# First maxima in every second expert of the last chunk, the mixed output's products split, and the second attention's first weights split in the gate's network

## What is computed

```python
xn = layernorm(x)
q, k, v = (split(lora_linear(xn, ...)) for ...)        # 16 heads of 16, full attention
s = lora_linear(softmax(q @ k.T * 0.25) @ v, Wo, ...)
x_lat = xn @ fc1.T                                     # mixture of 32 experts, 8 per token
h = relu2(einsum('tl,eil->eti', x_lat, w1)) * cw
routed = einsum('eti,eli->tl', h, w2) @ fc2.T
shared = relu2(xn @ shared_up.T) @ shared_down.T
x = x + s * silu(shared + routed)
xn = layernorm(x)
s = attention(xn)                                      # 32 heads of 64, 30 of them local, 2 global
x = x + s * silu((sigmoid(xn @ Q(w1).T) * (xn @ Q(w2).T)) @ Q(w3).T)   # Q: ternary weights
```

## Time and profile before

| | us |
|---|---|
| median of 3 runs | 3155.75 (3152.42 to 3157.56) |
| the profiled execution | 3153.2 |
| its span, first to last instruction | 3151.4 |
| PE busy in it | 3000.4 (95%) |
| DVE, ACT, POOL busy | 2127.0 (67%), 1864.5 (59%), 993.8 (32%) |
| stage 1 (`first_half`) | 0 to 684.4 |
| stage 2 (`first_attention`) | 684.4 to 1449.0 |
| stage 3 (`gate_network`) | 1449.0 to 1626.5 |
| stage 4 (`second_attention`) | 1626.5 to 3151.4 |

### The profile page before, as it was taken

One profiled execution on the slowest core, in us unless ns is written; L12 is line 12 of the kernel. 1 busy time (PEld: TensorE's weight loads), 2 busy tenths in 40 slices (PEclk: granted clock), 3 DMA queues, 4 the chain that ended last, 5 costly groups with the idle time before them and its releaser, 6 DMA issues. The chain is left out here.

```text
span 3151.4 us, 66399 instructions
## 1 busy us (share of the span) xinstructions
PE 3000.4 (95%) x23634; PEld 2263.2 (72%) x23634; DVE 2127.0 (67%) x5897; ACT 1864.5 (59%) x4638; POOL 993.8 (32%) x1607
## 2 busy tenths in 40 slices
PE   7999999989999999996988999999999999999998
PEld 5888888854444444434877888788887888788886
DVE  5666666679989989976755555555556555565556
ACT  4666666648877777783435555455554555545553
POOL 0000000000000000002016666576655766566663
PEclk9999999989999999998999999999999999999999
DMA  4111111142233143102224444354343444244432
GB/s 150 49 48 48 48 48 41 44 84 41 54 50 70 29 76 47 30 7 100 97 83 109 104 95 96 98 127 103 83 118 88 117 103 93 66 116 108 101 87 69
DMA packets 296707, 246.35 MB, mean 78 GB/s; under 512 B 149180, under 2 KB 231740, under 8 KB 296252
## 3 DMA queue, kind: packets, MB, share of 16 engines
q1 hardware_dynamic: 296380, 242.11, 31.7%
HBM read 100.71 MB, written 44.04 MB: 46 GB/s over the span
## 5 line engine op out<-in xcount | busy, mean ns | idle before, releaser
L1804 ACT ACTIVATE b_pp<-b_pp,b_nm 128x192 f32<-128x192 f32 (+2 forms) x1024 | 472.9, 463 | 448.5 <-DVE b_nm L1972 367.0
L974 ACT ACTIVATE a_pt<-ps 128x512 f32<-128x512 f32 x1024 | 556.1, 595 | 169.8 <-PE ps L1006 168.8
L176 DVE TENSOR_REDUCE mx<-ps 128x2 f32<-128x1024 f32 x512 | 621.4, 1224 | 50.7 <-PE ps L167 36.3
L1774 POOL TENSOR_SCALAR b_pp<-b_pp,b_rc 128x192 f32<-128x192 f32 x960 | 388.6, 432 | 383.4 <-DVE b_rc L1981 383.4
L1993 DVE COPY b_pt<-ps 128x384 f32<-128x384 f32 (+2 forms) x336 | 182.0, 555 | 317.7 <-PE ps L1893 302.4
L1972 DVE CUSTOM_DVE_ANT_0 b_pp<-ps,b_mk 128x192 f32<-128x192 f32 x960 | 276.4, 354 | 133.4 <-PE ps L1872 133.4
L800 DVE SCALAR_TENSOR_TENSOR f_yac<-ps,f_cw,f_yac 128x128 f32<-128x128 f32 x992 | 278.1, 343 | 128.1 <-PE ps L604 125.7
L959 POOL TENSOR_TENSOR a_s<-a_s,g 128x256 f32<-128x256 f32 x32 | 23.4, 731 | 879.0 <-DVE a_s L1070 879.0
L604 PEld LDWEIGHTS ps<-w,f_sq 128*128 128x128 f32 x2048 | 265.7, 191 | 25.4 <-issue 5.1
L604 PE MATMUL ps<-w,f_sq 128*128 128x128 f32 x2048 | 269.7, 275 | 0.3
L1927 PE MATMUL ps<-b_wo,b_oT 128*128 128x256 f32 x1024 | 241.6, 380 | 3.7 <-ACT b_vv L1797 3.7
(11 more groups left out here) (269 smaller groups left out, 7310.6 us busy)
## 6 DMA issues: line engine op xcount, KB each, us to landing
b_rt<-b_qf SPq DMA_DIRECT2D x1024, 64.0 KB, 2.0
qk_parts<-f_aa SPq DMA_DIRECT2D x32, 512.0 KB, 2.7
v_rows<-f_va_ SPq DMA_DIRECT2D x16, 512.0 KB, 2.8
b_raw<-in_W1qT SPq DMA_DIRECT2D x64, 128.0 KB, 2.6
b_raw<-in_W1kT SPq DMA_DIRECT2D x64, 128.0 KB, 2.7
b_vraw<-in_W1vT SPq DMA_DIRECT2D x32, 256.0 KB, 3.2
b_wo<-in_W1oT SPq DMA_DIRECT2D x16, 512.0 KB, 4.0
b_vs<-b_vv SPq DMA_DIRECT2D x60, 128.0 KB, 2.8
```

The costliest lines, as they stand in the source:

```text
L176: e.tensor_reduce(M["mx"][kh % 3][:, :, jt, h], P.pair(s), AX.X, ALU.max, negate=True).then_inc(P.free_sem(s), 1)
L974: e.activation(pt[(4 * i + 2 * j + a) % 12][:, :], P.ap((*s, a)), ACT.Exp).then_inc(P.free_sem((*s, a)), 1)
L1774: m = e.tensor_scalar(x, x, r[:, 2 * u + h:2 * u + h + 1], 1.0, ALU.mult, ALU.mult)
L1804: e.activation(x, x, ACT.Exp, bias=nm[n % 4][:, c:c + 1], scale=-1.0, accum_out=sm[n % 4][:, c:c + 1]).then_inc(exp_done, 1)
```

## The change

**Stage 1.** Thirteen maxima lie inside the last chunk, one in every second expert from 7 to 31, and six behind it; `BEGUN` is 19. The twentieth is the first step of stage 2, whose rule counts from BEGUN + 1, so that all later slots have what they had. Unit 0 is loaded into `xh`/`xl` by the step `ahead` at expert 6, which waits only for the last reader of `xh`; unit 1 goes to `w1_h`/`w1_l` at expert 16 after `up` 15; unit 2's buffers are the second half of the experts' weights (`w1b`). `mix_part` is replaced by `mix_up` (the four shared matmuls of 128 tokens, which need no `yT`) and `mix_end` (the two `yT` x `fc2` matmuls), and the six maxima, `tail_turn`, `mix_up` and `mix_end` take turns; the maxima behind the chunk use banks 0, 1 and 6, 7.

```diff
-    begin = (19, 21, 23, 25, 27, 29, 30, 31)
+    begin = range(7, E, 2)
...
-                if c == NCH - 1 and e in (14, 16):
-                    p.append(("ahead", e // 2 - 7))
+                if c == NCH - 1 and e in (6, 16):
+                    p.append(("ahead", e // 16))
...
-    maxima(2)
-    p.append(("tail_turn", last))
-    maxima(1)
-    p.append(("mix_part", last, 0, 0))
-    maxima(2)
-    p += [("mix_part", last, 0, 1), ("mix", last, 0)]
-    maxima(2)
-    p.append(("mix_part", last, 1, 0))
-    maxima(2)
-    p += [("mix_part", last, 1, 1), ("rows", 0), ("mix", last, 1)]
-    maxima(3)
-    return p
+    p += [("mix_up", last, 0, 0)] + maximum(0)
+    p += [("tail_turn", last)] + maximum(1)
+    p += [("mix_up", last, 0, 1), ("mix_end", last, 0)] + maximum(2)
+    p += [("mix", last, 0), ("mix_up", last, 1, 0)] + maximum(3)
+    p += [("rows", 0)] + maximum(4)
+    p += [("mix_up", last, 1, 1)] + maximum(5)
+    return p + [("mix_end", last, 1), ("mix", last, 1)]
...
-                x = 3 * (n_max % 2) if s[1] >= in_chunk else 0
+                x = 6 * (n_max % 2) if s[1] >= in_chunk else 0
...
-        n = min(slot + 24, BEGUN + slot * 10 // 8, 32 * units)
+        n = min(slot + 24, BEGUN + 1 + slot * 10 // 8, 32 * units)
...
-    p += [("score", 0, j) for j in range(2)]
+    p += ahead(0) + [("score", 0, j) for j in range(2)]
```

```diff
+            p += [("load_ahead",), ("keep",)]
+        if i == 3:
+            p.append(("ahead",))
...
+                elif k == "ahead":
+                    w.wait_ge(M["raw_in"], 32)
+                    e.activation(M["wh"][0], M["raw"], ACT.Copy).then_inc(M["w_high"], 1)
+                    w.wait_ge(M["vraw_in"], 16)
+                    e.activation(M["vh"][0], M["vraw"], ACT.Copy).then_inc(M["v_high"], 1)
...
-    p += [("w_high", 0), ("w_low", 0, 0), ("w_low", 0, 1), ("v_high", 0), ("v_low", 0, 0), ("v_low", 0, 1)]
...
         def pool(e):
             w = Waits(e)
+            for z in vb + vs:
+                e.memset(z[:, :, :], 0.0).then_inc(pads, 1)
...
-            w.wait_ge(c_in, 80)
+            w.wait_ge(c_in, 32)
```

More of the change, by code:

```diff
@@ L255, in first_half_plan, with maximum @@
     last = NCH - 1
-    more = iter(range(len(begin), BEGUN))
-    def maxima(n):
-        for _ in range(n):
-            x = next(more)
-            p.append(("max", x))
-            if x == 15:
-                p.append(("both", 0))
-    maxima(2)
-    p.append(("tail_turn", last))
-    maxima(1)
-    p.append(("mix_part", last, 0, 0))
-    maxima(2)
-    p += [("mix_part", last, 0, 1), ("mix", last, 0)]
-    maxima(2)
-    p.append(("mix_part", last, 1, 0))
-    maxima(2)
-    p += [("mix_part", last, 1, 1), ("rows", 0), ("mix", last, 1)]
-    maxima(3)
-    return p
+    def maximum(n):
+        x = len(begin) + n
+        return [("max", x), ("both", 0)] if x == 15 else [("max", x)]
+    p += [("mix_up", last, 0, 0)] + maximum(0)
[5 more added lines that the diff above has]
+    return p + [("mix_end", last, 1), ("mix", last, 1)]
 def first_half(nc, A, M, X):
@@ L300, in first_half @@
             ww=[128, 4, E], sm=[128, 4], rc=[128, 4]).items()}
-        rl = [sb(f"rl{i}", [128, CH]) for i in range(2)]
+        rl = M["rl"]
         sq = [sb(f"sq{i}", [128, CH]) for i in range(4)]
@@ L329, in first_half @@
             elif s[0] == "rows":
-                P.take(s, 6)
-            elif s[0] == "mix_part":
+                P.take(s, 4)
+            elif s[0] == "mix_up":
                 if s[3] == 0:
-                    P.take(("mix", *s[1:3]), 5 if s[2] == 0 else 2)
+                    P.take(("mix", *s[1:3]), 2 + s[2])
             elif s[0] in ("tail_turn", "mix") and s[1] == NCH - 1:
                 if s[0] == "tail_turn":
-                    P.take(s, 2)
+                    P.take(s, 5)
             elif s[0] in ("w_lora", "turn", "gate", "gate_turn", "latent", "qk", "values", "shared", "tail_turn", "mix"):
@@ L615, in tensor @@
                     for i in range(2):
-                        m = mixed(s, i)
+                        mix_up(s, i)
+                        m = mix_end(s, i)
                     m.then_inc(P.full_sem(s), 1)
-                elif k == "mix_part":
-                    mix, i = ("mix", c, s[2]), s[3]
-                    w.wait_ge(*P.before(mix))
+                elif k == "mix_up":
+                    mix = ("mix", c, s[2])
+                    for ready in P.all_before(mix):
+                        w.wait_ge(*ready)
                     w.wait_ge(hs_ready, 4 * (c + 1))
+                    mix_up(mix, s[3])
+                elif k == "mix_end":
+                    mix = ("mix", c, s[2])
                     w.wait_ge(*P.emptied(("tail_turn", c)))
-                    m = mixed(mix, i)
-                    if i == 1:
-                        m.then_inc(P.full_sem(mix), 1)
+                    for i in range(2):
+                        m = mix_end(mix, i)
+                    m.then_inc(P.full_sem(mix), 1)
                 elif k == "max":
@@ L1202, in pool @@
                                     ALU.is_lt).then_inc(is_neg_1, 1)
+                elif s[0] == "ahead":
+                    for i in range(2):
+                        w.wait_ge(M["w_high"], 1)
+                        e.tensor_tensor(M["wl"][0][:, i, :], M["raw"][:, i, :], M["wh"][0][:, i, :].bitcast(F32),
+                                        ALU.subtract).then_inc(M["w_low"], 1)
+                        w.wait_ge(M["v_high"], 1)
+                        e.tensor_tensor(M["vl"][0][:, i, :], M["vraw"][:, i, :], M["vh"][0][:, i, :].bitcast(F32),
+                                        ALU.subtract).then_inc(M["v_low"], 1)
         def scalar(e):
@@ L2036, in build @@
             "rows_in": [[ctx.enter_context(nc.semaphore(f"rows_in{i}{h}")) for h in range(2)] for i in range(3)],
+            "rl": [sb(f"rl{i}", [128, CH]) for i in range(2)],
+            "xt": sb("xt", [128, 2, 4, 256]),
             "v0_in": ctx.enter_context(nc.semaphore("v0_in")),
@@ L2042, in build @@
         }
+        for n in ("c_in", "raw_in", "vraw_in", "w_high", "w_low", "v_high", "v_low"):
+            M[n] = ctx.enter_context(nc.semaphore(n))
+        w1b = [sb(f"w1b_{n}", [128, E // 2, 128], FR) for n in "hl"]
+        for i, n in enumerate("hl"):
+            for j, x in enumerate("wv"):
+                M[x + n] = [w1b[i][:, 8 * j + 4 * k:8 * j + 4 * k + 4, :].rearrange("p (c a) b -> p c (a b)", c=2)
+                            for k in range(2)]
+        M["cos"], M["sin"] = (M["xt"][:, i, :, :].rearrange("p a b -> p (a b)") for i in range(2))
+        M["raw"], M["vraw"] = (x[:, :].rearrange("p (c o) -> p c o", c=2) for x in M["rl"])
         with ExitStack() as c0:
```

71 lines of the change are left out of this document (35 added, 36 removed).

## The result

| | us |
|---|---|
| after, median of 19 runs | 3149.57 (3139.51 to 3166.57) |
| before, median of 19 runs beside them | 3157.56 (3150.70 to 3164.07) |
| ratio | 0.9969, 95% interval 0.9957 to 0.9980 |
| profiled execution of after | 3151.62, span 3149.8 |

Forecast were 3145 and a gain of 10.6; measured are 3149.6 and, by the two medians, a gain of 8.0. The range of 3138 to 3151 holds the median, and the whole interval lies at 0.2% or more under before, if only just.

The account below looks back on a forecast made before the run. PE, busy 95% of the span, was taken as the bound, with gains left at the seams between stages. Terms -6.4 + 0.4 + 0.1 - 4.7 = -10.6 us, from the median 3155.75 to 3145 us; range 3138 to 3151.

Parts of the forecast that it names:

- Six maxima inside the chunk: Stage 1, last chunk: six more maxima before expert 29, each costing 0.63 us of PE time; +3.8 us.
- The DMA wait goes: Stage 1, maximum at expert 19: PE's wait for the load of q and k disappears; -1.3 us.
- From expert 29 to the seam: End of stage 1: from expert 29's maximum to stage 2 takes 18.5 us against 27.4; -8.9 us.
- Parts 1 to 3: Stage 1: extra maxima, removed DMA wait and shorter way from expert 29 to the seam together give -6.4 us.
- The twentieth maximum: Start of stage 2: PE's two matmuls ahead of the first scores cost between 0 and +0.4 us, taken as +0.4.
- The clock at the start of stage 2: First steps of stage 2: PE's lower clock costs as much as before; between 0 and -5 us, taken as 0.
- slower: Start of stage 2: lower clock stays down 34 us longer, some 50 in all, making +6.3 and 3162 us; chance 0.04.
- The rival by which the full clock would be carried over the seam: Stage 1 to stage 2: the shorter PE gap keeps full clock, 5 us lower, 3140 us; chance 0.14.
- Stage 3: Added loads and splits in stage 3 hold DVE, and PE behind it; +0.1 us, between 0 and +1.
- Stage 4: Start of stage 4: PE starts without splits and its third values product comes at T + 7.95, not T + 12.66; -4.7 us.

Follow-up runs that it names:

- fewer: after plus 7 unread fp32 matmuls of 128 rows: 3 behind stage 1's last product, 4 ahead of the second to fourth score pairs; 3139.2 us, ratio 0.9944.
- full_seam: after plus 16 unread reduced-fp32 matmuls of 48 rows: 7 behind stage 1's last product, 9 ahead of the second to fourth score pairs; 3149.7 us, ratio 0.9977.
- recover: after plus 12 unread fp32 matmuls of 128 rows, three ahead of each of the maxima 22 to 25 in stage 2; 3149.7 us, ratio 0.9970.
- before_filled: before plus 13 unread fp32 matmuls of 128 rows: 8 behind stage 1's last product, 5 ahead of the second to fourth score pairs; 3154.0 us, ratio 0.9992.

## Why the prediction came out as it did

By its own steps:

1. *Six maxima inside the chunk*, +3.8: as rebuilt, 3.81 us for two experts and a maximum.
2. *The DMA wait goes*, -1.3: gone.
3. *From expert 29 to the seam*, 18.5 us forecast, 18.9 measured. Parts 1 to 3 together: -6.4 forecast, -6.0 by the two profiles; the kernels with the old first half end stage 1 at 683.3 to 684.4, those with the new one and no fillers at 677.4 to 678.4.
4. *The twentieth maximum*, +0.4 with 0 as its lower end: 0 by the first Exp.
5. *The clock at the start of stage 2*, between 0 and -5, taken as 0: **this term failed.** The profiled execution has +8.2 us. The step in the text was "Now PE is idle only about 2 us ahead of the seam" and "I take 0, since the gaps of the first steps are made by ACT and stay": it took the 16 or 17 us of one execution for a property of the kernel and asked only whether the stretch would get shorter. It had no term for a length that varies from 17 to 41 us in the unchanged kernel. And the argument against the rival "slower", that the clock "came back as soon as PE was steadily busy", rested on the two seams of that one execution; in after the profile has TensorE busy without a gap from 690 to 710, at the lower clock. By the Trainium skill (TensorE: Matmul & The Clock Gate, Part 1: The HAM clock gate) activity releases the throttle; this trace doesn't bear that out for these matmuls. The rival by which the full clock would be carried over the seam named a time that does occur (3140; six executions of after at a mean clock of 0.991 have 3139.5 to 3141.8, and `fewer` gives 3139.2), but its condition does not hold: the shorter gap did not carry the clock over the seam in the profile of after, nor did the absence of any gap over 0.45 us in that of `full_seam`. That the 0 was nearly right for the average all the same (about 1 us, see below) is luck: nothing in the prediction said that the stretches of the two kernels would be about equally long.
6. *Stage 3*, +0.1, bounds 0 to +1: +0.3 by the two profiles, and 0 to +3.1 in the others, where a stretch of 3.4 or 6.8 us at the lower clock stands between 1481 and 1499 in all that took over 1 us more, in kernels with and without the splits. ACT's two copies of 0.62 us and POOL's splits stood where the forecast had them, and TensorE's wait for the product of that chunk is 1.36 us instead of 1.17, 0.2 us more where 0.1 was forecast.
7. *Stage 4*, -4.7: -3.4 by the two profiles; 1524.2 to 1525.6 with the old start, 1519.1 to 1523.7 with the new (x not in pieces), -3.7 in the mean. The instants at its start were hit within 0.5 us (`vraw`'s issue by 0.5, TensorE's by 0.1), and 4.3 us were still there after a sixth of the stage; 0.9 us went later, in small steps whose cause is open.

The size, then. The schedule gains some 10 us, and the clock decides how much of it is seen in one execution. After's 19 runs fall into seven at a mean clock of 0.990 or 0.991 (3139.5 to 3141.8 us), eleven at 0.984 to 0.987 (3148.8 to 3153.8) and one at 0.980 (3166.6); the median is in the middle group, which has the mean clock of the profile (0.987). Where the executions without a profile were at the lower clock is not known; that it was seam one is inferred from the profiles. An estimate from the mean clocks (0.9878 over 19 executions of after, 0.9863 over 94 of before), less the other stretches of the two profiles (42.7 and 54.9 us), gives an average of 34 us at seam one for after and 31 us for before, thus about 1 us of the 2.6 that the medians miss. The rest, and whether the new schedule really makes the stretch longer, is within what these runs scatter; by the ratio (9.8 us) hardly anything is missing. Of the 4.6 us between forecast and median another 1.8 are before's own median, which was 3157.56 in this comparison and 3155.75 in the one that the forecast started from.

The rival *slower* was this mechanism, priced at 0.5 us for a microsecond and with 34 us more needed. Measured were 0.38 us, and the stretch was 20 us longer in the profile and about 3 in the mean, by the estimate above.

## What to carry to other kernels

Before a term of a forecast is taken from one profile, ask whether the thing itself varies: the mean granted clock listed with every execution says so at once, and sorting executions by it separates a good part of the clock's share from the schedule's. Not all of it: at 0.987 after lies 4.4 us under before (nine executions of each), since the change also took away some of before's lower clock elsewhere, and two executions with one mean clock need not have lost it at one place. At a change of stage where TensorE goes over to small matmuls, a few fp32 matmuls with an unread result can be worth more than a good schedule: seven of them gave 8 us here by the ratios and 10 by the medians, about as much as the whole change. Place them where TensorE waits anyhow, since those that stood ahead of scores or maxima at full clock were paid for, and where the clock is still up: at the lower clock, in `recover` and `before_filled`, it came back within 4 us of the first of them, but they took 0.7 to 0.8 us each instead of 0.46.
